# A decoder layer on one core: the convolution from shifted copies, two taps a product, and the FFN weight kept in float32 with its column scales inside

## The reference

```python
proj = einsum('blh,he->bel', x, W_in); hidden, gate = split(proj)     # 1024 channels each
hidden = silu(causal depthwise convolution with 4 taps (hidden) + conv_bias)
dt, Bm, Cm = split(hs @ W_x)                                          # 128, 16, 16
dts = softplus(dt @ W_dt + b_dt);  A = -exp(A_log)
state = exp(dts*A)*state + dts*Bm*hs;  y = sum_n(state*Cm)            # 16 states a channel
x = layernorm(x + ((y + hidden*D) * silu(gate)) @ W_out)
x = layernorm(x + x @ softmax(q(ctx) k(ctx)^T)^T)
w_q = round(weight / w_scale)                    # w_scale = rowmax|weight| / 127
x_q = round(x / x_scale)                         # x_scale = rowmax|x| / 127
x = layernorm(x + (x_q @ w_q^T) * x_scale * w_scale + bias)
```

## Time and profile before

| what | value |
| --- | --- |
| median of 3 runs | 1060.97 us (1060.91 to 1061.49) |
| the profiled execution, its own time | 1060.82 us |
| its span, first to last instruction | 1059.0 us |
| mean granted TensorE clock | 0.913 of full speed |
| busy in the span: DVE, PE, ACT, POOL | 984.8, 864.7, 806.3, 734.5 us |
| chain that ended last, by engine | DVE 32%, issue 31%, PE 18%, ACT 13% |

### The profile page before, as it was taken

How to read it: one execution, slowest core, us unless ns; L and a number is a source line. 1 busy time by engine, 2 the same in 40 slices (tenths; PEclk the granted TensorE clock), 3 DMA queues, 4 the chain that set the end, 5 groups by cost and what they waited for, 6 DMA issues and landing times.

```text
span 1059.0 us, 10554 instructions
## 1 busy us (share of the span) xinstructions
PE 864.7 (82%) x3078; PEld 352.8 (33%) x3088; DVE 984.8 (93%) x813; ACT 806.3 (76%) x1222; POOL 734.5 (69%) x260
## 2 busy tenths in 40 slices
PE   8955788876899899977699899967799576767895
PEld 3321233321344343322244344432234242323432
DVE  3699999999999999899999999899999999999747
ACT  4486788876778898998767898997876886986424
POOL 1057777777787766688778866588778867878443
PEclk9988799888899999978899999989799879878998
DMA  6255444554743344343744544344743443244001
GB/s 197 78 125 133 102 120 129 122 132 115 196 126 88 101 129 119 80 116 102 231 125 100 129 120 109 79 106 130 213 115 90 133 106 90 70 129 110 1 0 40
DMA packets 58473, 120.08 MB, mean 113 GB/s; under 512 B 12208, under 2 KB 18480, under 8 KB 58416
## 3 DMA queue, kind: packets, MB, share of 16 engines
q1 hardware_dynamic: 57696, 119.34, 43.0%
q10 hardware_dynamic: 720, 0.08, 0.1%
HBM read 48.07 MB, written 4.19 MB: 49 GB/s over the span
## 4 chain that ended last, share of the span: by engine, by line
DVE 32%; issue 31%; PE 18%; ACT 13%; DMA 2%; SPq 2%; POOL 2%; DVEq 0%; POOLq 0%; ACTq 0%
DVE st L784 21%; PE dense L897 10%; DVE dBu L776 7%; ACT dA L553 4%; PE dense L944 3%; ACT L553 2%; DMA rep<-steps 2%; PE dense L975 2%; SPq L357 1%; POOL st L447 1%; ACT L543 1%; DVE dense L880 1%; DVE xsc L840 1%; PE dense L926 1%; PE dense L919 1%
## 5 line engine op out<-in xcount | busy, mean ns | idle before, releaser
L447 POOL TENSOR_TENSOR st<-st,Cb 128x2048 f32<-128x2048 f32 x127 | 649.4, 5113 | 266.8 <-DVE dBu L776 265.9
L784 DVE TENSOR_TENSOR_SCAN st<-dA,dBu 128x1024 f32<-128x1024 f32 x256 | 570.1, 2266 | 0.4 <-ACT dA L553 0.4
L553 ACT ACTIVATE dA<-rep,Aneg 128x511 f32<-128x511 f32 x512 | 328.2, 710 | 53.7 <-DVE st L784 49.4
L776 DVE TENSOR_TENSOR dBu<-rep,Bb 128x1024 f32<-128x1024 f32 x256 | 305.2, 1236 | 1.9 <-DMA rep<-steps 1.9
L897 PE MATMUL dense<-xTs,Win 128*128 128x512 f32 x504 | 237.0, 617 | 7.9 <-ACT wide L558 5.1
L944 PE MATMUL dense<-st,sel 128*32 128x512 f32 x1024 | 139.2, 691 | 57.7 <-POOL st L447 57.0
L897 PEld LDWEIGHTS dense<-xTs,Win 128*128 128x128 f32 x504 | 99.8, 200 | 137.5 <-issue 136.8
L897 PE MATMUL dense<-wide,hs 128*128 128x512 f32 x256 | 114.7, 601 | 1.9 <-DVE hs L750 1.0
L553 ACT ACT_TABLE_LOAD x78 | 100.1, 1283 | 9.7 <-DVE st L784 8.5
L975 PE MATMUL dense<-pj,Win 128*128 128x512 f32 (+1 forms) x192 | 87.6, 599 | 1.7 <-ACT pj L529 0.9
L944 PEld LDWEIGHTS dense<-st,sel 128*32 128x32 f32 x1024 | 33.4, 124 | 158.3 <-issue 89.8
(11 more groups left out here) (120 smaller groups left out, 778.7 us busy)
## 6 DMA issues: line engine op xcount, KB each, us to landing
rep<-steps SPq DMA_DIRECT2D x512, 128.0 KB, 2.4
Win<-w_in SPq DMA_DIRECT2D x64, 256.0 KB, 2.9
wide<-w_out SPq DMA_DIRECT2D x4, 2048.0 KB, 9.7
Win<-w_conv SPq DMA_DIRECT2D x24, 256.0 KB, 2.9
xTs<-xT SPq DMA_DIRECT2D x3, 1024.0 KB, 5.7
x<-x SPq DMA_DIRECT2D x3, 1024.0 KB, 8.5
out<-x SPq DMA_DIRECT2D x12, 256.0 KB, 2.0
wide<-w_x SPq DMA_DIRECT2D x4, 640.0 KB, 5.0
```

What stands on the lines that cost most here:

```text
L447: nc.gpsimd.tensor_tensor(s, s, Cb[:], ALU.mult).then_inc(s_p, NH)
L553: nc.scalar.activation(dA[:, u % 2, j, 1:T], rep[:, u % REPS, 0, 1:T], ACT.Exp, scale=Aneg[:, u % UNITS, j:j + 1]).then_inc(s_dA, 1)
L776: V.tensor_tensor(dBu[:, j, :], rep[:, u % REPS, 1:2, :].to_broadcast([P, JH, T]), Bb[:, j, :], ALU.mult).then_inc(s_mul, 1)
L784: V.tensor_tensor_scan(st[:, u % RING, j, :].rearrange("p j t -> p (j t)"), dA[:, u % 2, j, :].rearrange("p j t -> p (j t)"), dBu[:, j, :] ...
```

## The change

- **Convolution.** After ACT's copy to `pj`, SP makes four DMAs (`shift_taps`): each half of 64 channels goes to partitions 0 to 63 of `pk[:, m]`, and once more, moved by one position, to partitions 64 to 127. A matmul then takes 128 rows (64 channels, two taps) to 64 columns; a `c` is four such matmuls, two for each half of the output partitions. SP waits in step g for the copy of that step's `h` and for the convolution before it; ACT's next copy to `pj` waits for the DMAs (`s_pk`). The convolution weights are half as large.
- **FFN.** `WfT` is float32 and holds integer times scale; `ws` and `ws_bc` are gone; `xqT` is float32; L880 is gone, the row scale goes into the operation that adds the rows. All `ff` matmuls are float32.
- **Order.** `y` is first in its step; `c` comes behind `h`, `xt`, `av`, `qt` and `ff`; the tables are changed.
- **Smaller.** `steps` has two buffers (`DTS`); `sel` is [128, 32]; `xsc`, `xinv` take the place of `wscale`, `winv`; of the last unit's product with C DVE makes the second half.

```diff
-REST = {"wo": [3, 3, 6, 8], "q": [2], "k": [1], "en": [5, 9, 10, 11], "at": [10, 12, 14, 14],
-        "xt": [13, 13, 14, 15], "av": [15, 17, 19, 19], "qt": [18, 20, 22, 23], "ff": [19, 22, 23, 25]}
-REST_BESIDE = {"q": [22], "k": [22], "en": [23, 23, 26, 27], "at": [26, 27, 28, 29], "wp": [27, 28, 29, 30]}
-REST_AFTER = {"wo": [3, 4, 5, 6], "xt": [5, 6, 7, 8], "av": [6, 7, 8, 9], "qt": [9, 10, 11, 12],
-              "ff": [10, 11, 12, 13]}
-HID_AT = [5, 9, 11, 13, 14, 17, 19, 22]
-CONV_AT = [9, 10, 13, 14, 17, 18, 21, 24]
+REST = {"wo": [3, 3, 6, 7], "q": [2], "k": [3], "en": [4, 7, 10, 11], "at": [9, 11, 13, 14],
+        "xt": [13, 14, 14, 17], "av": [15, 17, 19, 19], "qt": [18, 20, 22, 23], "ff": [21, 22, 23, 25]}
+REST_BESIDE = {"q": [22], "k": [22], "en": [23, 24, 25, 26], "at": [26, 27, 29, 30], "wp": [27, 29, 29, 30]}
+REST_AFTER = {"wo": [3, 3, 4, 6], "xt": [5, 6, 7, 8], "av": [6, 7, 8, 9], "qt": [9, 10, 11, 12], "ff": [10, 11, 12, 15]}
+HID_AT = [6, 9, 12, 13, 14, 16, 18, 21]
+CONV_AT = [9, 10, 13, 14, 16, 19, 21, 24]
...
+            def shift_taps(b, i):
+                n = NE * (b - 1) + i
+                product_read(sp, ("h", b, i))
+                if n:
+                    product_done(sp, ("c", (n - 1) // NE + 1, (n - 1) % NE))
+                else:
+                    sp.wait_ge(s_prep, 1)
+                for m in range(2):
+                    half = slice(64 * m, 64 * m + 64)
+                    sp.dma_start(pk[0:64, m, :], pj[half, :]).then_inc(s_pk, 16)
+                    sp.dma_start(pk[64:128, m, 1:T], pj[half, 0:T - 1]).then_inc(s_pk, 16)
...
                 if n:
-                    product_done(act, ("c", (n - 1) // NE + 1, (n - 1) % NE))
+                    act.wait_ge(s_pk, 64 * n)
                 nc.scalar.copy(pj[:], ps).then_inc(free, 1)
...
+            def weigh_last_states():
+                u = NB * UNITS - 1
...
+                dve.wait_ge(s_p, NH * u + 1)
+                s = st[:, u % RING, JH:NJ, :]
+                V.tensor_tensor(s, s, Cb[:, JH:NJ, :], ALU.mult).then_inc(s_p, 1)
...
-                    rounded(x1[:, i, :], x1[:, i, :], winv[:, i:i + 1]).then_inc(s_wq, 1)
...
+                    link(rounded(x1[:, i, :], x1[:, i, :], winv[:, i:i + 1]))
+                    V.tensor_scalar(x1[:, i, :], x1[:, i, :], ROUND, wscale[:, i:i + 1], ALU.subtract,
+                                    ALU.mult).then_inc(s_wq, 1)
...
-                        link(V.scalar_tensor_tensor(ps, ps, xsc[:, i:i + 1], ws_bc[:], ALU.mult, ALU.mult))
                         dve.wait_ge(s_xb, TT * kb + i + 1)
-                        add_rows(key, x_i, ps, free)
+                        add_rows(key, x_i, ps, free, xsc[:, i:i + 1])
...
-                        product_read(pe, ("h", kb, i))
+                        pe.wait_ge(s_pk, 64 * (NE * (kb - 1) + i + 1))
                         ps, done = bank_of(key)
-                        for k in range(KC):
-                            mm = nc.tensor.matmul(ps[:, k:T], Win[:, n % 3, k, :], pj[:, 0:T - k],
-                                                  start=k == 0, stop=k == KC - 1)
+                        for k in range(0, KC, 2):
+                            for m in range(2):
+                                mm = nc.tensor.matmul(ps[64 * m:64 * m + 64, k:T],
+                                                      Win[:, n % 3, k // 2, 64 * m:64 * m + 64],
+                                                      pk[:, m, 0:T - k], start=k == 0, stop=k == KC - 2)
```

More of the change, by code:

```diff
@@ L30 @@
 REPS = 4
+DTS = 2
 RING = 6
@@ L82, in rest @@
             keys.extend((kind, kb, i) for i, at in enumerate(table.get(kind, ())) if at == g)
+    if g % 4 == SUM_AT and 0 <= n - 1 < NB * NE:
+        keys.append(("y", (n - 1) // NE, (n - 1) % NE))
     if after and g == (B_AT if b >= 0 else 27):
@@ L91, in items @@
         keys.append(("z", (n + 2) // NE, (n + 2) % NE))
-    if after and b >= 0:
-        keys.extend(("c", b + 1, i) for i, at in enumerate(CONV_AT) if at == g)
     if after:
@@ L99, in items @@
         rest(b, REST_BESIDE, ("q", "k", "at", "en", "wp"))
+    if after and b >= 0:
+        keys.extend(("c", b + 1, i) for i, at in enumerate(CONV_AT) if at == g)
     if after and g == DT_AT:
@@ L172, in decoder_layer @@
         winv = sb("winv", [P, KH])
-        ws_bc = sb("ws_bc", [P, H])
         xTs = sb("xTs", [P, 2, KH, T])
         hs = sb("hs", [P, 2, NE, T])
-        steps = sb("steps", [P, 3, 2, T])
+        steps = sb("steps", [P, DTS, 2, T])
         rep = sb("rep", [P, REPS, 2, T])
@@ L233, in decoder_layer @@
         s_act_c = sem("act_constants_loaded")
+        s_pk = sem("conv_taps_loaded")
         s_wx = sem("wx_loaded")
@@ L376, in _ @@
                         load_w(wuse.index(key) + 3)
+                for key in items(b, g):
+                    if key[0] == "h" and key[1]:
+                        shift_taps(*key[1:])
                 if scanned and g == 2 and b + 1 < NB:
@@ L429, in _ @@
                                     base=0, pattern=[[-1, P]], channel_multiplier=1).then_inc(s_masks, 1)
-            for n, d in enumerate(range(-3, 4)):
+            for n, d in enumerate(range(-3, 1)):
                 if n:
@@ L448, in weigh_states @@
                 else:
[L449 to L452, removed]
+                    pool.wait_ge(s_scan, NH * u + 1)
+                    s = st[:, u % RING, 0:JH, :]
+                    nc.gpsimd.tensor_tensor(s, s, Cb[:, 0:JH, :], ALU.mult).then_inc(s_p, 1)
             rows = []
@@ L539, in soft @@
                 ps, free = full(("z", b, e))
-                if n >= 3:
-                    act.wait_ge(s_dA, NJ * NQ * (n - 2))
-                    act.wait_ge(s_du, n - 2)
-                nc.scalar.activation(steps[:, n % 3, 0, :], ps, ACT.Softplus, bias=bdt[:, e:e + 1]).then_inc(free, 1)
+                if n >= DTS:
+                    act.wait_ge(s_dA, NJ * NQ * (n - DTS + 1))
+                    act.wait_ge(s_du, n - DTS + 1)
+                nc.scalar.activation(steps[:, n % DTS, 0, :], ps, ACT.Softplus, bias=bdt[:, e:e + 1]).then_inc(free, 1)
             def exps(u, j):
@@ L707, in rounded, with add_rows @@
                 return V.tensor_scalar(dst, src, inverse, ROUND, ALU.mult, ALU.add)
-            def add_rows(key, x_i, ps, free):
+            def add_rows(key, x_i, ps, free, scale=1.0):
                 n = norm[key]
@@ L758, in step_inputs @@
                 hidden_ready(dve, b, e)
-                if n >= 3:
-                    for v in range(NQ * (n - 3), NQ * (n - 2)):
+                if n >= DTS:
+                    for v in range(NQ * (n - DTS), NQ * (n - DTS + 1)):
                         dve.wait_ge(s_rep[v % REPS], 64 * (v // REPS + 1))
-                V.tensor_tensor(steps[:, n % 3, 1, :], steps[:, n % 3, 0, :], hs[:, b % 2, e, :],
+                V.tensor_tensor(steps[:, n % DTS, 1, :], steps[:, n % DTS, 0, :], hs[:, b % 2, e, :],
                                 ALU.mult).then_inc(s_du, 1)
@@ L1013, in _ @@
                         turned(key, x1[:, i, :])
-                    elif kind == "ws":
-                        pe.wait_ge(s_wq, KH + 1)
-                        ps, done = bank_of(key)
-                        for k in range(KH):
-                            mm = nc.tensor.matmul(ps[:, k * P:(k + 1) * P], wide_scale[:, k, :], ident[:],
-                                                  start=True, stop=True)
-                        mm.then_inc(done, 1)
                     elif kind in ("wp", "wo"):
@@ L1075, in columns @@
         return v.reshape(-1, P).T
-    taps = np.zeros((NE, P, KC, P), np.float32)
+    taps = np.zeros((NE, 2, 64, 2, P), np.float32)
     for k in range(KC):
-        taps[:, range(P), k, range(P)] = a["attn_conv_kernel"][:, 0, KC - 1 - k].reshape(NE, P)
+        w = a["attn_conv_kernel"][:, 0, KC - 1 - k].reshape(NE, 2, 64)
+        for m in range(2):
+            taps[:, k % 2, range(64), k // 2, range(64 * m, 64 * m + 64)] = w[:, m]
+    taps = taps.reshape(NE, P, 2, P)
     arrays = {
```

47 lines of the change are left out of this document (21 added, 26 removed).

## The result

The changed kernel took 1048.03 us (median of four runs, 1045.81 to 1049.92); beside it the kernel before took 1061.23. The ratio is 0.9872, with an interval of 0.9858 to 0.9887: 1.3% faster. The profiled execution took 1045.81 us, the fastest of the four, with a span of 1044.0; it is 15.0 us shorter than the span of before, while the medians are 13.2 apart.

A forecast was written before the change was run, and what follows sets the result against it. DVE alone sets the pace where no earlier sequence's rest runs; beside a rest DVE and PE both do, ACT close behind. 1060.8 - 8.9 - 5.8 - 6.1 - 0.4 + 4.0 + 1.0 = 1044.6 us, range 1030 to 1055.

The forecast's parts named there:

- The scale operation, 8.9: FFN on DVE: dropping L880 twelve times between units, at 0.738 us each, wins 8.9 us.
- `y` first, 6.1: Sequence 3: the state sum first in its step removes DVE's 6.12 us wait at 993.40; 6.1 us won.
- Convolution, PE side: Each `c` on PE falls from 3.59 to 1.8 us with paired halves, 2.0 if width changes cost 0.25.
- Convolution, shift: From ACT's copy of `h` to the tap's arrival by four SP DMAs: 4.8 us, with 2.4 and 7 as ends.
- a limit a few microseconds off: Slower rival, chance 0.07: from some 7 us a shift, exponentials are delayed; at 8.2 us 25 lost, 1069.8.
- Sequences 1 and 2, 2.9 each: DVE waits there: 9.2 us go, 6.3 of stalls come; 2.9 won in each, 5.8 in all.
- The stall of 2.0 for ACT: Sequence 1, step 15: exponentials start at 396.6, so DVE wants the first two at 396.1 and gets them at 398.0.
- The 3.76 for `ff0`: DVE's wait for the first `ff` in sequence 1 goes, since `ff0` is two steps later; 3.76 us.
- DVE's half of the last product, 0.4: Last unit's product with C: only PE's 0.40 us wait for the second half goes; 0.4 won.
- Bank and slow clock in sequence 3, 1.0 lost: Sequence 3: `ff2` waits for `ff1`'s bank and may meet a slow clock; 1.0 us more.
- The tail, 4.0 lost: After the last scan, float32 `ff` make PE the chain; `ff3` ends at 1056.9, last L714 was at 1052.98; 4.0 lost.
- The signs: DVE busy down by some 12 us would show the prediction right; DVE idle in sequence 0 would show it wrong.

The follow-up runs named there:

- the repeated run: The changed kernel run once more without any edit, beside the other experiments; median 1047.64 us, ratio 0.9868 to the kernel before.
- the first two experiments: Changed kernel with convolution and FFN both of before (order, tables and DVE's half left): 1056.52 us; changed kernel with only the convolution undone: 1057.55 us.
- the first experiment: Changed kernel with the convolution and FFN of before, leaving the order, tables and DVE's half of the last product: 1056.52 us, ratio 0.9953.

## Why the prediction was right

Foretold were 1044.6 us, 1030 to 1055, faster; the profiled execution, against which the sum was made, took 1045.81, and the median was 1048.03. The changed kernel's runs spread over 4 us (1045.8 to 1049.9) where those of before beside them spread over 1.5. Part of that is the waits for `ff2`, which go with the clock (2.31 and 1.59 in the fastest execution, 3.20 and 2.08 in the repeated run of 1047.46). The kernel with GpSimd's two halves, the same up to the last unit, was profiled at 1050.34: DVE waits 4.1 us more there before the last scan, 2.1 of them for `ff2`. The executions near 1049.9 have no trace, so for them the cause stays open.

The sum stood close to the fastest execution, and its parts on DVE's own timeline mostly came. As an account of what each edit is worth it was off by several microseconds both ways, and that these cancel is luck: the FFN was booked 3 to 5 too high, and the halves are worth 2 to 4 more than the 5.8 booked for sequences 1 and 2, order and all.

- **The scale operation, 8.9.** It went as booked. The adds that took over the row scale cost 0.03 to 0.06 more each, 0.5 between the units, which the prediction had at nothing.
- **`y` first, 6.1.** 5.9 came. But the step named half of the cause: first in its step alone makes the kernel 2 us slower. "The `wp` behind them are then needed a step later" is true only of the new table, which the prediction read but didn't book. The pair gives 4 to 5 in the kernel of before.
- **Convolution, PE side.** 1.8 for a `c` was 1.94, or 1.87 to the start of the next, at the full clock; at half of it, 3.67. Around it the width changes: of two products of full width the second starts 3.44 us after the first (395.83, 399.27); where a change of width lies ahead of the first it is 3.54 (427.77, 431.31), where one lies behind it too, 3.63 (403.79, 407.42). So a change is some 0.1 us, and the 0.25 for two was about right (the 3.42 in it stands in none of its rows). By the Trainium skill's rule (TensorEngine Tiling (Array Packing), Key Properties: a change of tiling mode drains TensorE) a `c` came to 2.0 at the trace's price, and this trace agrees. The 2.3 scaled from the Trainium skill's three column tiles (TensorE: Matmul & The Clock Gate, Part 3) was too high; the trace shows nearly the full factor, though not by what means.
- **Convolution, shift.** 4.8 us from ACT's copy to the tap: the trace shows 4.3 for `c2`. The four issues take 2.4 us, and the last begins 1.8 after the copy and has landed 2.5 later; the prediction added issue and landing end to end. That there is a limit a few microseconds off was right: eight shorter shifts cost 19 us, mostly through the convolution's weights.
- **Sequences 1 and 2, 2.9 each.** 3.3 and 3.8 came, from partly other waits. `y2` and the normalization went, `y3` is out at 403.86 (foretold 404.8) and `y4` is waited for 1.23 (1.9). The stall of 2.0 for ACT didn't come: ACT had copied `h2` at 376.6 (foretold 377.2), the shift took 4.3 instead of 4.8, and the exponentials started at 395.05 (396.6), for a scan at 397.11. The 3.76 for `ff0` went as foretold. In place of the stall stands a wait for `ff2` (2.31), on a slow clock, for which the prediction had nothing. It looked at a slow clock only for sequence 3. There the clock fell too (0.51 from 918 to 921 us), and `ff1` took 5.2 us, but DVE didn't wait for it.
- **DVE's half of the last product, 0.4:** 0. PE was the later one.
- **Bank and slow clock in sequence 3, 1.0 lost.** 0: the only wait of DVE there is 0.27.
- **The tail, 4.0 lost.** 4.1, in its place: the last add is 48.1 us behind the end of the last scan, where it was 44.1.

```profile
1030.22 0.75 DVE L728 SCALAR_TENSOR_TENSOR hs<-dense,wscale,hs 128x512 f32<-128x512 f32 x1 [0.96 <-PE dense L916]
...
1037.90 0.75 DVE L728 SCALAR_TENSOR_TENSOR hs<-dense,wscale,hs 128x512 f32<-128x512 f32 x1 [1.50 <-PE dense L916]
```

- **Not in the sum:** 2.0 us more in dBu, and 1.1 before the first scan, which differs from run to run (53.8 to 55.2 us over these kernels).
- **The signs.** DVE's busy time fell by 6.7 and not by some 12: of the 11.8 of the scale operations, dBu took back 2.0, half of the last product 1.2, the second operation of `round_weight` 1.2 and the adds 0.7. DVE idle in sequence 0 was named as a sign of being wrong; the first trace has none, the repeated run's has 0.75 at a state sum.

What the working hid is where the gain sits. It booked 8.9 less 4.0 and 1.0 to the FFN, and treated the convolution as near balance on PE. With the new order throughout, the four kernels are:

| median us | convolution at full width | in halves |
| --- | --- | --- |
| FFN in bfloat16, scales on DVE | 1056.52 | 1048.30 |
| FFN in float32 | 1057.55 | 1048.03, 1047.64 |

The order is worth 5 against before, nearly all of it in sequence 3; the halves 8.2 to 9.9; the FFN between -1.0 and 0.7. The expectations of the first two experiments were drawn from the same booking: the first was 7.5 us too low, the second 7.5 below even at the upper end of its range.

Open: why some dBu pairs take 2.9 to 3.5 us instead of 2.36. There are five in the trace of before and seven in the changed kernel's (ten in that of the first experiment), mostly at the same place in each sequence. Nothing was tried on it. The best version here is the changed kernel with `h2` a step earlier, 1043.3 us, or 1043.0 with `h7` moved too; the two can't be told apart.

## What to carry to other kernels

Where PE, ACT and DVE are all nearly full in a stretch, price a shorter product by what stands behind it in the queue of the engine that reads it, not by the engine's own spare time; here the halves were worth 8 to 10 us, most of it in shorter waits at the state sums and for ACT. An operation taken off the bound engine was worth next to nothing, because what made it needless lengthened the tail and a product that the same engine waits for. A reordering and the table that goes with it are one edit, and half of it can cost time. Before adding a DMA between two products, look at what its issue pushes back in the issuing queue, the inputs of that very product included, and place the producer one step earlier.

## What was not expected of the hardware

- Four matmuls of 64 columns take 1.94 us whether the two halves alternate or not, where four of 128 columns take 3.59.
- After 5.12 us without work a float32 product took 5.83 us (6.20 and 6.72 in other runs) instead of 3.6 to 3.7, at a granted clock of 0.50. A wait thus costs more than its length, on the product that everybody waits for. `c1` of sequence 1 shows it as well: nearly twice its time after 3.88 us, at 0.50.

```profile
356.41 3.67 PE L995 MATMUL dense<-pk,Win 128*64 128x512 f32 x8 [3.88 <-issue]
```

- Halving the shift DMAs brought each to its place only 0.3 us sooner (2.0 instead of 2.3), and 2.4 us of issue time were added for it.
